# Two graph attention layers with a mixture of experts: five unread products ahead of each pair of lookups

## The chip, the cores and the metric
The kernel runs on one core of one Trainium2 chip. The metric is the device time in microseconds (us), median of several runs. TensorE does matrix products (MATMUL, each with a weight load, LDWEIGHTS), VectorE and ScalarE elementwise work, GpSimd gathers rows by indirect DMA, SyncE issues the other DMAs. Products are written to PSUM, eight banks of 512 float32 columns.

## The reference
```python
x = x + gnn(layernorm(x), edge_index, ...)    # graph 1: 6250 nodes, 100000 edges, 8 heads
x = x + ffn(layernorm(x), ...)                # graph 2, and four experts of which two count

# ffn: scores from a second graph attention over 131072 edges and self loops
e = leaky_relu(a_src[src] + a_dst[dst]); ee = exp(e - e_max[dst])
alpha = ee / segment_sum(ee, dst)[dst]
agg = segment_sum(h[src] * alpha, dst)        # 16 values a node: 4 heads x 4 experts
scores = layernorm(agg).mean(over heads); w = softmax(top 2 of scores)
for ei in range(4):
    out += g[ei] * (gelu(x @ W1[ei] + b1[ei]) @ W2[ei] + b2[ei])   # 256 -> 512 -> 256
```

## The kernel before
The kernel goes through graph 1's features and edges, a middle part that makes graph 2's node table, graph 2's edge stage, and an output stage. Only graph 2's edge stage is touched (`p_edges2` on TensorE, and its partners `v_edges2`, `a_edges2`, `g_edges2`, `sp_edges2` on the other engines).

Graph 2's edges lie in 656 chunks of 128. A round is `W2` = 16 chunks, so there are 41 rounds; `CH` is 4 and u = 0 to 3 names a quarter of a round. Each round has 16 slots, and every engine runs the same loop over rounds and slots, each with its own instructions, ordered by semaphore counts. Into the slots, besides the edge work, the steps of the experts' feed-forward network are dealt out evenly (`ffn_at`): an "up" product (float32, 512 columns, L1354) of which two make the input of one GELU on ScalarE (L858), and a "down" tile (four float32 products of 256 columns, L1368), which VectorE evacuates three slots later (`LATE` = 3, L2570) with the count v_y. A down tile waits until the tile before last is evacuated. The node groups are of 4 tiles, the last one of 1 tile, whose up products have 128 columns.

The edge work of round i on TensorE:
- in each slot one sum product for a chunk of round i - 2 (L1398, bfloat16, 60 columns), which needs VectorE's one-hot matrices (v_oh, L2581) and messages (v_ms);
- in slots 8 and 12, twice a round, `lookups` for two quarters of round i: per chunk one bfloat16 product of 24 columns (L1382) that gives each edge its destination's terms, eight products a time. They are written to columns 0 to 383 of bank i % 2. They need table rows that ScalarE copied in the round before (a_tw, L872), one-hot matrices that VectorE made of rows loaded by DMA (v_st, L2590, at its slots 0 and 4), and the bank, free once VectorE has read it for round i - 2 (v_z, the score at L2596).

GpSimd gathers a chunk's 128 source rows per instruction (L728), up to three rounds ahead, and every four chunks waits for TensorE's sums. VectorE adds the sums into the accumulator (L2642). SyncE stores the evacuated tiles (L512) and loads the destination rows (L519).

`ident` and `ones` are float32 128x128 constants in SBUF. All float32 products appear in the trace as two MATMULs and two LDWEIGHTS each.

Of the kernel before, what the change touches and what calls it, by code (L numbers as in the profile page):

```python
# [42 lines left out]
def build(nc, x_d, src_d, dst_d, W_d, as_d, ad_d, bias_d, lns_d, lnb_d, Wg_d, gas_d, gad_d, bg_d, gam_d, bet_d,  # L43
# [8 lines left out]
    with ctx:  # L52
        def sb(name, shape, dt=f32):
            return ctx.enter_context(nc.sbuf_tensor(name, shape, dt))

        def pb(name, shape, dt=f32):
            return ctx.enter_context(nc.psum_tensor(name, shape, dt))
# [4 lines left out]
        def sems(names):  # L62
            return [sem(n) for n in names.split()]
# [68 lines left out]
        ident = sb("ident", [128, 128])  # L132
        ident16 = sb("ident16", [128, 128], b16)
        tri = sb("tri", [128, 128])
        ones = sb("ones", [128, 128])
# [52 lines left out]
        pbank = [pb(f"pb{i}", [128, 512]) for i in range(8)]  # L188
# [149 lines left out]
        def wait_read(e, n):  # L338
# [19 lines left out]
        l_d1, s_dlT, v_oT, p_tp, a_w32, p_ad, v_z, a_ex, v_msg, p_sum, v_add = sems(  # L358
            "l_d1 s_dlT v_oT p_tp a_w32 p_ad v_z a_ex v_msg p_sum v_add")
# [113 lines left out]
        def ffn_at(n):  # L473

            return [op for s in ffn_steps[taken[n]:taken[n + 1]] for op in s] if n >= 0 else []
# [867 lines left out]
        def p_ffn(pe, op):  # L1343
            if op[0] == "up":
                _, bi, f, k = op
                ei, gi = blk[bi]
                t0, nt = groups[gi]
                n, w, b = 4 * bi + f, ei % 2, 5 + (4 * bi + f) % 2
                if k == 0:
                    if f == 0 and gi == 0:  # L1350
                        pe.wait_ge(l_w1[w], 32 * (ei // 2 + 1))
                    if n >= 2:
                        pe.wait_ge(a_gel, n - 1)
                t = pe.matmul(pbank[b][:, 0:nt * 128], W1s[:, w, k, f * 128:f * 128 + 128],  # L1354
                              xT[:, t0:t0 + nt, k * 128:k * 128 + 128], start=k == 0, stop=k == 1)
                if k == 1:
                    t.then_inc(p_up, 1)
            if op[0] == "down":
                _, bi, j = op
                ei, gi = blk[bi]  # L1360
                n, w = downs[(bi, j)], ei % 2
                b = (4, 7)[n % 2]
                if n >= 2:
                    pe.wait_ge(v_y, n - 1)
                for f in range(4):
                    if j == 0:
                        pe.wait_ge(a_gel, 4 * bi + f + 1)
                    t = pe.matmul(pbank[b][:, 0:D], hh[:, bi % 2, f, j * 128:j * 128 + 128], W2s[:, w, f, :], start=f == 0, stop=f == 3)  # L1368
                t.then_inc(p_dn, 1)

        def p_edges2(pe, m, lo, hi, base, fill):
            nf = 0

            def lookups(n):
                i, u = divmod(n, 4)
                r = i - base
                pe.wait_ge(m["a_tw"], n - 4 * base + 1)
                pe.wait_ge(m["v_st"], 2 * r + u // 2 + 1)
                if r >= 2:
                    pe.wait_ge(m["v_z"], 4 * (r - 2) + 1)  # L1380
                for k in range(u * CH, u * CH + CH):
                    t = pe.matmul(pbank[i % 2][:, 24 * k:24 * k + 24], ST2[:, k // 8, k % 8, :], tabw[:, i % 2, 24 * k:24 * k + 24],  # L1382
                                  start=True, stop=True)
                t.then_inc(m["p_ad"], 1)

            for i in range(lo, hi + 2):
                for u in range(4):
                    for k in range(CH):
                        c = (i - 2) * W2 + u * CH + k
                        if c >= lo * W2:  # L1390
                            rc = c - base * W2
                            if u == 0 and k == 0:
                                pe.wait_ge(m["v_ms"], 6 * (i - 2 - base) + 6)
                            if k == 0:
                                pe.wait_ge(m["v_oh"], 4 * (i - 2 - base) + u + 1)
                            if rc >= 16 and rc % 8 == 0:
                                pe.wait_ge(m["v_wh"], rc // 8 - 1)
                            pe.matmul(pbank[2 + c // 8 % 2][:, c % 8 * 60:c % 8 * 60 + 60], S2[:, i % 2, u * CH + k, :],  # L1398
                                      Mb[i % 2][:, u * CH + k, :, :], start=True, stop=True).then_inc(m["p_sm"], 1)
                        if k == 0 and u >= 2 and i < hi:  # L1400
                            lookups(4 * i + 2 * u - 4)
                            lookups(4 * i + 2 * u - 3)
                        if fill:
                            for op in ffn_at(nf):
                                p_ffn(pe, op)
                            nf += 1

        def tensor_program(pe):
# [107 lines left out]
            for step in ffn_steps[0:PRE2]:  # L1516
                for op in step:
                    p_ffn(pe, op)
            p_edges2(pe, main2, 0, ROUNDS, 0, True)


# [1209 lines left out]
```

## Time and profile before

| | us |
|---|---|
| time, median of 3 runs (2254.3 to 2259.53) | 2255.82 |
| profiled execution, span from first to last instruction | 2627.5 |
| profiled execution, its own time beside the span | none is given; the span stands for it |
| TensorE, MATMUL busy in the span | 1983.2 |
| VectorE busy | 1730.8 |
| GpSimd busy | 1554.8 |
| ScalarE busy | 871.5 |
| graph 2's edge stage, about | 1505 to 2521 |

The profiled execution is 372 us longer than the median of the runs. Times in the rows are of the profiled execution. Engines are named PE (TensorE matmul), PEld (its weight loads), DVE (VectorE), ACT (ScalarE), POOL (GpSimd) and SP (SyncE); an "L" and a number is the line of the kernel. "Idle before" is the time that an engine did nothing ahead of an instruction, with what released it; "issue" is time in which it waited for nothing that the profile shows, "remote" a release that no instruction of the trace accounts for.

### The profile page before, as it was taken

Reading aid. Unit: us, or ns where it says so; the run is one execution under the profiler, and the core shown is the slowest. Engines: PE = TensorE matmul, PEld = TensorE weight load, DVE = VectorE, ACT = ScalarE, POOL = GpSimd, SP = SyncE. Lnnn points to the kernel's source line nnn. Section 1 sums busy time; section 2 is a strip of 40 time slices with the busy share of each in tenths; the row PEclk is TensorE's granted clock in tenths of the full one; section 3 lists DMA queues with packets and bytes.
Section 4 is the critical chain, followed back from the end, with each engine's and each line's share of the span. In section 5 each row is a group of like instructions: output and inputs, shape, how many; then the busy total and the mean of one; then the engine's idle time right before and its main releaser. Section 6 shows DMA issues by size and latency. Waiting matters only on the chain.

```text
span 2627.5 us, 36265 instructions
## 1 busy us (share of the span) xinstructions
PE 1983.2 (75%) x10396; PEld 1276.1 (49%) x10396; DVE 1730.8 (66%) x4885; ACT 871.5 (33%) x2296; POOL 1554.8 (59%) x1720
## 2 busy tenths in 40 slices
PE   7577675677778677777777668788788788888857
PEld 5243354445445444544545435454455455555536
DVE  6588897778888888888599225444444454454568
ACT  6311111333333333333266323333323233233225
POOL 2666676666666666667464546666565666566600
PEclk9789987899999899998778679899888998899978
DMA  7434444434434443434600112222122222221137
GB/s 211 129 101 111 111 121 111 113 107 108 113 108 108 113 111 106 112 108 111 201 5 7 26 48 60 55 75 58 47 55 70 54 63 63 51 38 35 32 125 272
DMA packets 147851, 239.99 MB, mean 91 GB/s; under 512 B 39734, under 2 KB 79332, under 8 KB 147652
## 3 DMA queue, kind: packets, MB, share of 16 engines
q0 software_dynamic: 58624, 116.81, 18.7%
q1 hardware_dynamic: 89028, 120.82, 14.8%
q8 instruction: 89, 1.46, 0.2%
q14 instruction: 110, 0.90, 0.1%
HBM read 203.79 MB, written 33.72 MB: 90 GB/s over the span
## 4 chain that ended last, share of the span: by engine, by line
PE 43%; DVE 17%; issue 15%; another core or an unknown queue 15%; ACT 4%; DVEq 2%; POOL 1%; DMA 1%; ACTq 1%; SPq 0%
PE pb L1451 9%; PE pb L1368 8%; PE pb L1354 8%; PE pb L1341 5%; PE pb L1333 2%; DVE x_sb L2497 1%; PE pb L1438 1%; PE pb L1529 1%; DVE Gb L1665 1%; PE pb L1299 1%; DVEq L2636 1%; DVE home L2642 1%; DVE x_sb L2406 1%; ACT x_sb L848 1%
## 5 line engine op out<-in xcount | busy, mean ns | idle before, releaser
L775 POOL DMA_INDIRECT Gb<-table,home x400 | 411.3, 1028 | 217.3 <-issue 95.2
L1368 PE MATMUL pb<-Gb,early 128*128 128x256 f32 x1568 | 436.1, 424 | 87.4 <-DVE home L2570 39.5
L1354 PE MATMUL pb<-big,Gb 128*128 128x512 f32 (+1 forms) x832 | 444.1, 648 | 70.0 <-issue 38.6
L1368 PEld LDWEIGHTS pb<-Gb,early 128*128 128x128 f32 x1568 | 311.7, 209 | 190.9 <-issue 79.5
L2497 DVE TENSOR_SCALAR x_sb<-iota,x_sb 128x394 bf16<-128x394 f16 x1024 | 349.2, 385 | 42.4 <-PE pb L1341 19.9
L858 ACT ACTIVATE early<-pb,b1c 128x512 f32<-128x512 f32 (+1 forms) x208 | 136.8, 662 | 634.9 <-remote 349.4
L1341 PE MATMUL pb<-x_sb 128*128 128x394 bf16 x1024 | 296.6, 349 | 12.8 <-DVE x_sb L2497 7.2
L728 POOL DMA_INDIRECT home<-table,idx x224 | 216.5, 966 | 151.2 <-issue 62.4
L2570 DVE TENSOR_TENSOR home<-pb,b2B 128x256 f32<-128x256 f32 x147 | 62.0, 422 | 363.1 <-remote 291.6
L728 POOL DMA_INDIRECT tab<-table,idx x224 | 219.1, 978 | 137.9 <-issue 61.2
L848 ACT ACTIVATE x_sb<-pb 128x512 f16<-128x512 f32 x256 | 153.0, 598 | 368.4 <-remote 151.9
L728 POOL DMA_INDIRECT early<-table,idx x208 | 200.0, 962 | 126.7 <-issue 55.6
L1451 PE MATMUL pb<-Gb,Sall 128*128 128x264 f32 x800 | 261.9, 430 | 7.2 <-DVE Gb L1665 3.6
L775 POOL DMA_INDIRECT home<-table,home x192 | 197.4, 1028 | 96.4 <-issue 47.5
L775 POOL DMA_INDIRECT early<-table,home x192 | 201.7, 1050 | 86.8 <-issue 48.9
L965 ACT CAST Sall<-pb 128x1024 f32<-128x1024 bf16 x98 | 99.1, 1012 | 350.3 <-PE pb L1438 188.8
L1354 PEld LDWEIGHTS pb<-big,Gb 128*128 128x128 f32 x832 | 135.9, 204 | 160.2 <-issue 122.8
L1333 PE MATMUL pb<-x_sb 128*128 128x512 f16 x256 | 104.4, 408 | 103.7 <-issue 46.8
L1451 PEld LDWEIGHTS pb<-Gb,Sall 128*128 128x128 f32 x800 | 159.9, 212 | 41.9 <-issue 11.8
L2642 DVE TENSOR_TENSOR home<-home,asall 128x20 f32 x656 | 116.1, 178 | 96.4 <-issue 50.7
L1665 DVE TENSOR_TENSOR Gb<-Gb 128x512 f32<-128x512 f32 x200 | 133.8, 685 | 33.3 <-ACT Gb L969 20.5
L1341 PEld LDWEIGHTS pb<-x_sb 128*128 128x128 f16 x1024 | 101.3, 102 | 101.3 <-DVE x_sb L2497 27.7
(455 smaller groups left out, 3590.5 us busy)
## 6 DMA issues: line engine op xcount, KB each, us to landing
Sall<-dlT SPq DMA_DIRECT2D x180, 256.0 KB
Y<-home SPq DMA_DIRECT2D x72, 256.0 KB
x_sb<-in_x_dram SPq DMA_DIRECT2D x5, 1536.0 KB, 20.2
Gb<-table,home POOLq DMA_INDIRECT x400
early<-Y SPq DMA_DIRECT2D x8, 768.0 KB, 5.7
out_dram<-x_sb SPq DMA_DIRECT2D x24, 256.0 KB
Gb<-Y SPq DMA_DIRECT2D x6, 768.0 KB, 8.6
Gb<-in_L_ffn_W_dram SPq DMA_DIRECT2D x8, 512.0 KB
```

The source lines that it names most:

```text
L728: g.indirect_dma_start(out=Gt2[s][:, k, :], out_offset=None, in_=g2.table, in_offset=bass.IndirectOffsetOnAxis(ap=g2.idx[:, c:c + 1], axis ...
L775: g.indirect_dma_start(out=G1[i % 4][:, k, :], out_offset=None, in_=g1.table, in_offset=bass.IndirectOffsetOnAxis(ap=g1.idx[:, c:c + 1], a ...
L848: a.activation(Av[g % 4], hot_bank[:, :], ACT.Relu).then_inc(a_av, 1)
L858: a.activation(hh[:, bi % 2, f, 0:nt * 128], pbank[b][:, 0:nt * 128], ACT.Gelu, bias=b1c[:, ei, f:f + 1]).then_inc(a_gel, 1)
L1333: pe.matmul(hot_bank[:, :], CT[g // 4 % 2], lanes[:, g % 4 * 512:g % 4 * 512 + 512], start=True, stop=True).then_inc(p_hot, 1)
L1341: pe.matmul(pbank[5 + 2 * w][:, 0:HW], A, Bv[n], start=j % HB == 0, stop=j % HB == HB - 1).then_inc(p_pl, 1)
L1354: t = pe.matmul(pbank[b][:, 0:nt * 128], W1s[:, w, k, f * 128:f * 128 + 128], xT[:, t0:t0 + nt, k * 128:k * 128 + 128], start=k == 0, stop ...
L1368: t = pe.matmul(pbank[b][:, 0:D], hh[:, bi % 2, f, j * 128:j * 128 + 128], W2s[:, w, f, :], start=f == 0, stop=f == 3)
L1451: pe.matmul(sbank[m % 3][:, 0:g1.R], S1[:, i % 2, k, :], G1[(i - 2) % 4][:, k, :], start=c % RUN == 0, stop=c % RUN == RUN - 1).then_inc(p ...
L1665: v.tensor_tensor(hv, hv, G1[e % 4][:, o, 256:264].unsqueeze(3).broadcast_to([128, 2, 8, 32]), ALU.mult).then_inc(v_msg, 1)
L2497: v.tensor_scalar(Bv[j % NB], iota16[:, 0:HW], winF[:, k:k + 1], bE[:, k:k + 1], ALU.is_equal, ALU.mult).then_inc(v_bv, 1)
L2642: v.tensor_tensor(o, o, sums2[c // 8 % 2][:, c % 8, :], ALU.add).then_inc(m["v_ad"], 1)
```

## The change
A helper `p_turn_over` does n float32 products of 128 columns, `ident` by `ones`, into columns 384 to 511 of a bank, which nothing reads. `lookups` calls it with n = 5 for u = 0 and u = 2, that is once ahead of each of the two sets of eight lookups in a round, on the bank that the lookups are about to write. The wait for the bank (v_z) is moved ahead of the products; the waits for the tables (a_tw) and the one-hot matrices (v_st) now come behind them. No semaphore is signalled by the products.

```diff
+        def p_turn_over(pe, bank, n):
+
+            for k in range(n):
+                pe.matmul(bank[:, 384:512], ident[:, :], ones[:, :], start=True, stop=True)
+
         def p_edges2(pe, m, lo, hi, base, fill):
             nf = 0
 
             def lookups(n):
                 i, u = divmod(n, 4)
                 r = i - base
+                if r >= 2:
+                    pe.wait_ge(m["v_z"], 4 * (r - 2) + 1)
+                if u in (0, 2):
+                    p_turn_over(pe, pbank[i % 2], 5)
                 pe.wait_ge(m["a_tw"], n - 4 * base + 1)
                 pe.wait_ge(m["v_st"], 2 * r + u // 2 + 1)
-                if r >= 2:
-                    pe.wait_ge(m["v_z"], 4 * (r - 2) + 1)
```

## Rows read from the trace of the kernel before

**Rows 1.** The page: span, busy times, granted clock in 40 slices (tenths)
```profile
span 2627.5 us, 36265 instructions
PE 1983.2 (75%) x10396; PEld 1276.1 (49%) x10396; DVE 1730.8 (66%) x4885; ACT 871.5 (33%) x2296; POOL 1554.8 (59%) x1720
...
PEclk9789987899999899998778679899888998899978
```

**Rows 2.** Windows: busy us (instructions) per engine, granted clock, DMA
```profile
1505.00:2521.00 1016.00, 833.60 (x3607) 512.82 (x3606) 470.46 (x1518) 328.56 (x960) 606.61 (x627) 0.89 0.23 52
```

**Rows 3.** The chain that ended last, 1505 to 2521 us, by line
```profile
by line: another core or an unknown queue 24.6%; PE pb L1354 20.8%; PE pb L1368 20.6%; issue 14.3%; DVEq L2636 2.2%; DVE home L2642 2.2%; ACT early L858 1.9%; PE pb L1382 1.0%; PE pb L1398 1.0%; ACT dl L872 1.0%; DVE home L2570 0.9%; DVE Sa
```

**Rows 4.** TensorE's waits, 1505 to 2521 us: total, times, longest
```profile
PE pb L1382 <- issue: 40.1, 30, 2.6
PE pb L1368 <- DVE home L2570: 39.5, 17, 6.8
```

**Rows 5.** Timeline of TensorE from 1522 us: start, us, what, idle before
```profile
1522.39 0.18 PE L1382 MATMUL pb<-dl,STb 128*128 128x24 bf16 x1 [2.62 <-issue]
...
1525.19 0.18 PE L1382 MATMUL pb<-dl,STb 128*128 128x24 bf16 x1 [2.62 <-issue]
```

**Rows 6.** Waits of all engines, 1505 to 2521 us: the longest two
```profile
ACT early L858 <- remote: 349.4, 58, 18.1
DVE home L2570 <- remote: 291.6, 42, 29.0
```

**Rows 7.** Timeline of TensorE, 1909 to 1928 us
```profile
1909.95 1.10 PE L1354 MATMUL pb<-big,Gb 128*128 128x512 f32 x2
1910.89 0.19 PE L1398 MATMUL pb<-iota,Sall 128*128 128x60 bf16 x1
...
1911.89 1.97 PE L1368 MATMUL pb<-Gb,early 128*128 128x256 f32 x8
1913.70 0.19 PE L1398 MATMUL pb<-tmr,Sall 128*128 128x60 bf16 x1
...
1923.88 3.78 PE L1368 MATMUL pb<-Gb,early 128*128 128x256 f32 x8 [4.07 <-DVE home L2570]
...
1927.53 0.39 PE L1382 MATMUL pb<-dl,STb 128*128 128x24 bf16 x8
```

**Rows 8.** Timeline of the other engines in the same stretch
```profile
1912.51 0.95 POOL L728 DMA_INDIRECT early<-table,idx  x1 [0.30 <-issue]
...
1923.40 0.42 DVE L2570 TENSOR_TENSOR home<-pb,b2B 128x256 f32<-128x256 f32 x1 [7.91 <-remote]
1923.56 0.69 ACT L858 ACTIVATE early<-pb,b1c 128x512 f32<-128x512 f32 x1 [5.04 <-remote]
1923.72 0.95 POOL L728 DMA_INDIRECT early<-table,idx  x1 [2.76 <-remote]
```

**Rows 9.** Groups by line and form in the stage; one line's durations and starts
```profile
L1368 PE MATMUL pb<-Gb,early 128*128 128x256 f32 x1523 | 425.7, 425 | 87.4 <-DVE home L2570 39.5 <-issue 28.3 <-DVE big L2570 9.9
L1354 PE MATMUL pb<-big,Gb 128*128 128x512 f32 x743 | 418.4, 674 | 40.0 <-issue 25.6 <-ACT early L858 14.3
...
L1354 PE MATMUL pb<-big,Gb 128*128 128x128 f32 x64 | 12.1, 326 | 11.0 <-ACT early L858 7.5 <-issue 3.5
...
L728 POOL DMA_INDIRECT tab<-table,idx x215: 941/947/1472, 1499.6 to 2499.9; - x108
```

**Rows 10.** Timelines with TensorE's float32 products of 128 columns
```profile
1750.36 1.20 PE L1354 MATMUL pb<-big,Gb 128*128 128x128 f32 x4
...
2516.38 0.19 PE L1398 MATMUL pb<-tmr,Sall 128*128 128x60 bf16 x1
2516.41 0.35 PE L1382 MATMUL pb<-dl,STb 128*128 128x24 bf16 x8
2516.61 0.69 PE L1354 MATMUL pb<-big,Gb 128*128 128x128 f32 x4
2517.14 0.19 PE L1398 MATMUL pb<-tmr,Sall 128*128 128x60 bf16 x1
```

## The prediction
> **What bounds the kernel now.** I read the page first: TensorE is busy 75% of the span, more than VectorE (66%) or GpSimd (59%), and the granted clock changes all along the span [rows 1]. An average over unlike stages says little, so next come the busy times by stage. The change acts only in graph 2's edge stage, 1505 to 2521 us. There TensorE is busy 833.6 of 1016 us, GpSimd 606.6, VectorE 470.5, at a mean granted clock of 0.89 [rows 2]. TensorE is the engine with least room, and 182 us of idle time is all the cover there is.
>
> Is that idle time where the products go, ahead of the lookups? The waits say: TensorE's idle time ahead of L1382 is 40.1 us in 30 pieces, and none is ended by a semaphore of ScalarE (a_tw) or VectorE (v_st); all is "issue" [rows 4]. The timeline shows what "issue" is: within one set of four or eight lookups, where nothing is waited for, single instructions come 2.80 us apart (1522.39, 1525.19) [rows 5]. Products ahead of the set can't fill gaps inside it. TensorE's waits on a semaphore are elsewhere, at the down products (L1368) for VectorE, 39.5 us in 17 pieces [rows 4].
>
> The chain of the stage gives 24.6% to "another core or an unknown queue" [rows 3], though one core runs. The waits name it: ScalarE's GELU waits 349.4 us and VectorE's evacuation 291.6 us for something without a releaser [rows 6]. The timeline shows one such case. TensorE begins the down product at 1911.89 and the next instruction at 1913.70, so it is through with it; VectorE, which evacuates it three slots later, starts only at 1923.40, ScalarE's GELU at 1923.56 and GpSimd's gather at 1923.72 [rows 7, 8]. Three engines that wait for three different TensorE counts go on within 0.32 us. So TensorE's completion signals reached them some 8 us late, and TensorE itself then stood 4.07 us for want of the evacuation [rows 7]. I read the stuttered issue and the late signals as one fault of TensorE's sequencer in this execution.
>
> That matters for how the profile stands to the clocked runs. The span is 2627.5 us, the median 2255.82: the profiled execution is 372 us (14%) longer. My terms are durations of warm, unstuttered stretches; the waits are what I trust least. If the 372 us come off evenly, the stage lasts 1016 x 2256/2627.5 = 872 us in a clocked run. A floor comes from GpSimd: 627 gathers [rows 2] at a start-to-start of 1.25 us [rows 8] are 784 us, and 21 us lie between its last gather at 2499.9 [rows 9] and the stage's end: 805 us. What TensorE must do at full clock, from start-to-start times: 743/2 = 371.5 up products of 512 columns x 0.94 us = 349; 1523/8 = 190 down tiles x 1.81 us = 345; 64/4 = 16 short pairs x 0.53 = 8; 656 sums x 0.03 = 20; 82 sets of eight lookups x 0.20 = 16 [rows 7, 9, 10]. Together 738 us. So in a clocked run TensorE has 67 to 134 us in the stage that it doesn't need, part of it idle and part of it lost at the low clock.
>
> **The change, part by part.** *The products.* W2 is 16 and there are 656/16 = 41 rounds, in each of which `lookups` is called with u = 0, 1, 2, 3; u = 0 and 2 issue five products each: 82 times five, 410 calls. A float32 call is two MATMULs and two LDWEIGHTS (the code has 32 short up calls in the stage, the trace 64 MATMULs of them [rows 9]), so 820 and 820 instructions. The same form stands in the trace: the last group's up products are float32 128x128 on 128 columns. Four MATMULs, two calls, go from 2516.61 to the next instruction at 2517.14, 0.53 us; a call is 0.265 us, five are 1.33 us. At the lower clock the four last 1.20 us instead of 0.69 (1750.36), five calls by that ratio 2.3 us [rows 10]. So 82 x 1.33 = **109 us** at full clock. Were 22% of them at 1.2 GHz (a granted mean of 0.89 between 1 and 0.5), 82 x (0.78 x 1.33 + 0.22 x 2.3) = 127 us. Bounds: by columns alone, from the 512-column call, 0.94/4 = 0.235 us a call and 96 us in all; with no overlap at all between instructions, the 0.326 us that a short MATMUL lasts on the mean [rows 9] ten times for each of 82 sets, 267 us. I take 109, since its row has the same form; ident and ones instead of activations change no size.
>
> The trace puts the cost of a short float32 MATMUL with its weight load at 0.13 us [rows 10]. The Trainium skill ("TensorE: Matmul & The Clock Gate", LDWEIGHTS) has a load take columns divided by 1.2 GHz, 107 ns here, pulled ahead of matmuls in flight. By that two loads bound a call at 0.21 us, and the sum would be 88 us instead of 109; the measured row decides.
>
> *The moved wait.* v_z is now waited for ahead of a_tw and v_st, and ahead of the products. It asks for the score of the round before last. VectorE makes the score of the last round in its slot 2, ahead of the evacuation of slot 3 that stands at 1923.40 [rows 8], and TensorE's next lookups come at 1927.53 [rows 7]; the score asked for is a whole round earlier still. Nothing waits: 0 us. Unread columns 384 to 511 of the same bank are written while VectorE reads, if at all, the other bank: 0 us.
>
> *The order.* The products stand ahead of the waits for a_tw and v_st, so they would cost nothing where TensorE waits there for over 1.3 us. No such wait is in the trace [rows 4], and the slots say why: TensorE asks for v_st at slots 8 and 12, VectorE issues the one-hots at its slots 0 and 4, and the tables were copied a round before. A VectorE more than eight slots late holds up TensorE earlier, at a down product, as it does at 1923.88 [rows 7]. So the products are pure work in TensorE's order. Behind them stand the lookups, the next sum and the next feed-forward step; the lookups' count is wanted by VectorE's score in the next round, and 1.3 us don't show there.
>
> *What absorbs them.* Delayed TensorE work eats idle time of its own that hangs on others (gathers, evacuations), not what is serial. Per round 2.7 us of products meet 67/41 = 1.6 to 134/41 = 3.3 us of room. With the stage at 805 us and half its 67 us of room of use, +109 - 34 = +75; all of it, +42; none, +109. With the stage at 872 us and half, +42; all, 847 against 872, nothing. Half of the smaller room is my choice, as the profiled execution's long waits are mostly its own: **+75 us, 2256 + 75 = 2331 us**, with 2290 to 2370 for this case.
>
> **The rivals.**
> *The clock repays it (faster).* The low clock comes after stalls, and in the stage it takes 22% of the time; what is lost by it is 0.11 x 1016 = 112 us here, 96 us scaled to a clocked run. If the products kept the clock up throughout and half of them lay in idle time, the sum would be -96 + 55 = -41, **2215 us**. It decides once more than 109 us less the hidden part comes back. For it: TensorE's low clock is real in the rows, 3.78 us for a down tile after a stall where a warm one takes 1.97 [rows 7]. Against it: the stalls of the trace lie ahead of down products, and the products come slots later. [...]
> *Absorbed (about the same).* GpSimd or late evacuations set the pace, with 872 us or more to the stage, and TensorE's 109 us go into its idle time: -5 to +25, **2265 us**. For it: 182 us of idle in the stage [rows 2]; against it: 14% of the span isn't there in clocked runs.
> *Dearer products.* Weight loads that don't overlap, 267 us less 34: +233, **2489 us**. Against it, the 0.53 us row.
>
> **How the numbers follow.** Likeliest case 0.70, clock 0.12, absorbed 0.13, dearer 0.05. Range 2255 to 2380: it takes in the likeliest case with 10 us above it and nearly all of the absorbed one, and leaves out the clock and the dearer case, under 2 in 10. No difference means within 0.2%, 4.5 us, about what can be told here: the absorbed case puts 0.05 within it and 0.08 above, and the others 0.01: faster 0.12, same 0.06, slower 0.82.
>
> **What would show it.** In the changed kernel's profile: 820 more short MATMULs, five calls in 1.3 us when warm, right behind the previous feed-forward step without idle time ahead of them; no semaphore wait ahead of L1382's successor; TensorE's busy time in the stage up by 100 to 130 us; the stage itself longer by half of that or more. The prediction is wrong if the granted clock of the stage rises from 0.89 to near 1 and the stage shrinks, or if busy time rises by 110 us and the time doesn't, which would make the real room far larger than 67 us.

## The result and the profile after

The changed kernel takes 2287.31 us against 2257.33 for the kernel before, medians of four runs each: a ratio of 1.0139, 95% interval 1.0117 to 1.0161, or +30 us. The direction is the forecast one and the time lies in the range, but the forecast step was +75 us, 2.5 times what came.

Of the page of the changed kernel, two of the lines that answer to [rows 1]:

```profile
span 2278.9 us, 37905 instructions
PE 1942.1 (85%) x11216; PEld 1290.0 (57%) x11216; DVE 1726.2 (76%) x4885; ACT 877.7 (39%) x2296; POOL 1568.6 (69%) x1720
```

The span is now 2 us below this execution's own time of 2280.76. There are 820 more MATMULs, 11216 instead of 10396. The profiled execution that the prediction rests on was 372 us longer than its kernel's clocked runs, so the two spans can't be compared. The kernel before was therefore profiled once more among the experiments. Its second profile has a span of 2244.8 us at a time of 2246.71, and all "before" below means that one.

The edge stage by windows, from some 2 us ahead of the first lookups to some 3 us behind the last, first the kernel before, then the changed one (columns as in [rows 2]):

```profile
1336.00:2140.00 804.00, 756.85 (x3624) 479.42 (x3623) 468.25 (x1523) 333.77 (x965) 611.98 (x631) 0.98 0.26 66
```
```profile
1336.00:2173.00 837.00, 836.62 (x4439) 567.67 (x4440) 478.96 (x1522) 332.33 (x960) 621.47 (x635) 1.00 0.27 64
```

The stage takes 33 us longer, and that is the whole difference. Before, TensorE is idle for 804 - 757 = 47 us of it, and the granted mean of 0.98 says that a little of the rest went at the lower of its two clocks. In the changed kernel it has no idle time and the full clock from end to end.

The chain of the stage, by line, the kernel before and the changed one:

```profile
by line: PE pb L1368 24.1%; PE pb L1354 23.2%; issue 20.3%; POOL early L728 9.6%; POOL home L728 9.1%; POOL tab L728 6.8%; PE pb L1382 1.2%; PE pb L1398 1.1%; DVEq L2636 0.9%; DVE home L2642 0.6%; DVE home L2570 0.5%; DVE big L2596 0.2%; AC
```
```profile
by line: PE pb L1354 42.7%; PE pb L1368 40.8%; PE pb L1374 11.6%; PE pb L1405 2.1%; PE pb L1389 1.8%; issue 0.2%; ACT L884 0.2%; ACTq L868 0.1%; DVE asall L2636 0.1%; DVE home L2649 0.1%; DVE early L2630 0.1%; DVE early L2626 0.1%; DVE home
```

Before, a quarter of the chain is GpSimd's gathers and a fifth is "issue": the 0.30 us from one gather to the next, and a wait of VectorE for the last gather of a round, which the next view shows. Afterwards it is TensorE alone, with 11.6% for the products (L1374; by the added lines L1382 is now L1389, L1398 is L1405, L2570 is L2577 and L2601 is L2608).

What a round of the kernel before waits for, in its timeline over all engines:

```profile
1715.74 0.19 PE L1398 MATMUL pb<-tmr,Sall 128*128 128x60 bf16 x1
...
1717.01 0.94 POOL L728 DMA_INDIRECT tab<-table,idx  x1 [0.30 <-issue]
...
1720.40 0.23 DVE L2601 TENSOR_TENSOR zc<-tab,big 128x64 f32<-128x64 f32 x1 [7.37 <-issue]
...
1722.40 0.42 DVE L2570 TENSOR_TENSOR home<-pb,b2B 128x256 f32<-128x256 f32 x1
...
1722.88 3.35 PE L1368 MATMUL pb<-Gb,early 128*128 128x256 f32 x7 [6.95 <-DVE home L2570]
```

GpSimd issues a round's last gather into `tab` at 1717.01. VectorE's score (L2601), the first reader of these rows, starts at 1720.40, 2.45 us after that gather has ended and after 7.37 us of waiting. "issue" in its row is no name of a releaser; that it is the gathers follows from the count (l_g) for which the code waits there, and from the experiments below, in which the wait grows with a slower GpSimd and is gone with fewer gathers. The evacuation behind it in VectorE's order comes at 1722.40, and TensorE, which ran out of allowed work at 1715.9, goes on at 1722.88. TensorE stands in slot 2 there. The products come in slots 8 and 12, so not in the wait itself; they only make TensorE come later to a place at which it had to wait for GpSimd. No run puts them in another slot.

The same wait in the groups of waits over the stage, the kernel before and then the changed one:

```profile
DVE zc L2601 <- issue: 89.6, 15, 7.4
DVE zb L2601 <- issue: 83.9, 16, 6.5
POOL home L728 <- issue: 61.3, 201, 0.3
```
```profile
DVE home L2577 <- PE pb L1368: 169.0, 100, 5.6
```

VectorE waited 173 us for gathers, in 31 of the rounds; now it waits for TensorE's down tiles, and no longer for gathers. In the first seven rounds of the kernel before it didn't wait for gathers either, because GpSimd starts ahead: the score comes 14 us behind its last gather at first, and 3 us in the seventh round. From the eighth on (1495 us) the head start is used up. GpSimd itself has no pause of more than 0.3 us ahead of a gather in this window, and its last gathers, in the kernel before and then in the changed one, start at nearly the same time (each line has the durations in ns, then the first and the last start in us):

```profile
L728 POOL DMA_INDIRECT tab<-table,idx x224: 940/944/1302, 1330.7 to 2146.2; - x112
```
```profile
L728 POOL DMA_INDIRECT tab<-table,idx x224: 941/947/1456, 1329.0 to 2149.8; - x112
```

So five products don't slow GpSimd; it is no longer what the stage waits for.

What one set of products costs, in TensorE's timeline of the changed kernel:

```profile
2163.87 1.36 PE L1374 MATMUL pb<-ones,ident 128*128 128x128 f32 x10
...
2165.07 0.35 PE L1389 MATMUL pb<-dl,STb 128*128 128x24 bf16 x8
```

Five products go from 2163.87 to 2165.07, 1.20 us, with no idle time in front; the mean of all 82 sets is 1.19. 82 x 1.20 = 98 us.

### The profile page after: what moved, and what is told of

It is laid out like the page before. It is cut to its first block, busy times and chain, and to the rows that moved or that the text cites. A ratio compares the mean times of both kernels' runs of the same rounds, so it can differ in the third digit from the quotient of the medians.

```text
span 2278.9 us, 37905 instructions
## 1 busy us (share of the span) xinstructions
PE 1942.1 (85%) x11216; PEld 1290.0 (57%) x11216; DVE 1726.2 (76%) x4885; ACT 877.7 (39%) x2296; POOL 1568.6 (69%) x1720
## 4 chain that ended last, share of the span: by engine, by line
PE 51%; DVE 20%; POOL 13%; issue 9%; DMA 5%; DVEq 1%; ACT 1%; ACTq 0%; SPq 0%
PE pb L1354 16%; PE pb L1368 15%; POOL Gb L775 6%; PE pb L1374 4%; PE pb L1458 3%; DVE x_sb L2504 3%; POOL home L775 3%; POOL early L775 3%; DMA Gb<-table,home 2%; PE pb L1341 2%; DVE Gb L1672 2%; PE pb L1536 2%; PE pb L1155 2%; DVE big L1636 1%; DVE x_sb L2413 1%
## 5 line engine op out<-in xcount | busy, mean ns | idle before, releaser
L775 POOL DMA_INDIRECT Gb<-table,home x400 | 419.4, 1048 | 126.5 <-issue 106.4
L1354 PE MATMUL pb<-big,Gb 128*128 128x512 f32 (+1 forms) x832 | 410.5, 608 | 10.5 <-DVE home L1796 9.6
L1368 PE MATMUL pb<-Gb,early 128*128 128x256 f32 x1568 | 385.3, 389 | 0.4 <-DVE home L2577 0.2
L2504 DVE TENSOR_SCALAR x_sb<-iota,x_sb 128x394 bf16<-128x394 f16 x1024 | 343.6, 384 | 0.0
L1368 PEld LDWEIGHTS pb<-Gb,early 128*128 128x128 f32 x1568 | 283.2, 190 | 81.9 <-issue 49.4
L1458 PE MATMUL pb<-Gb,Sall 128*128 128x264 f32 x800 | 248.6, 412 | 16.9 <-DVE Gb L1672 16.7
L2577 DVE TENSOR_TENSOR home<-pb,b2B 128x256 f32<-128x256 f32 x147 | 62.2, 423 | 180.8 <-PE pb L1368 180.8
L1458 PEld LDWEIGHTS pb<-Gb,Sall 128*128 128x128 f32 x800 | 152.0, 203 | 44.8 <-DVE Gb L1672 18.9
L1354 PEld LDWEIGHTS pb<-big,Gb 128*128 128x128 f32 x832 | 126.5, 192 | 84.3 <-issue 67.2
L1458 PE MATMUL pb<-early,Sall 128*128 128x264 f32 x384 | 120.1, 416 | 13.9 <-DVE early L1672 13.9
```

The source lines that it names most:

```text
L775: g.indirect_dma_start(out=G1[i % 4][:, k, :], out_offset=None, in_=g1.table, in_offset=bass.IndirectOffsetOnAxis(ap=g1.idx[:, c:c + 1], a ...
L1458: pe.matmul(sbank[m % 3][:, 0:g1.R], S1[:, i % 2, k, :], G1[(i - 2) % 4][:, k, :], start=c % RUN == 0, stop=c % RUN == RUN - 1).then_inc(p ...
L2504: v.tensor_scalar(Bv[j % NB], iota16[:, 0:HW], winF[:, k:k + 1], bE[:, k:k + 1], ALU.is_equal, ALU.mult).then_inc(v_bv, 1)
```

## The experiments

Three theories were put to the test. Theory A: GpSimd's gathers set the pace of the stage before, TensorE has some 66 us of room at full clock (804 less the 738 us of work counted in the prediction), the products fill it first, and cost their full time beyond. Theory B: a fixed share of each product is serial, which gives the same 30 us at five. Theory C, that the clock repays part of the products, would show with few of them.

**The kernel before, profiled again** (no edit).

> The kernel before, profiled once more. Theory A (GpSimd's gathers set the pace of graph 2's edge stage, and TensorE has some 70 us of idle time there at full clock): a profile without the stuttered issue and the late signals, span near 2256 us, the stage about 805 us long, GpSimd's gathers at an even 1.22 us, TensorE busy some 730 us at a granted clock of 1.0, its idle time in small pieces once a round ahead of a down product or a sum. Theory B (TensorE's own serial chain sets the pace, with cold stretches): the same span, but a granted clock in the stage well below 1 and GpSimd with idle time of its own.

One run, 2246.71 us. The profile is the one used above: no stuttered issue, gathers mostly 1.25 us apart (0.94 and 0.30 of it between) and 1.27 on the mean, where 1.22 was expected, TensorE idle for 47 us, nearly all of it in 27 waits at down tiles. That is theory A's picture with two misses: TensorE is busy 757 us and not 730, at a clock of 0.98 and not 1.0, which is still not well below 1; and its idle time is in fewer and longer pieces, up to 6.9 us.

**Other numbers of products.** The wait is moved in all of them; n is 0, 2, 3, 4, 5 or 10. They ran in three groups, each with its own runs of the kernel before.

```diff
-                    p_turn_over(pe, pbank[i % 2], 5)
+                    p_turn_over(pe, pbank[i % 2], 10)
```

> The wait for the bank moved ahead and no products. Every theory: no difference that can be measured, within 0.2%; if the moved wait had a price of its own, it would show here.

> Two products ahead of each set of lookups instead of five: 82 x 2 x 0.266 = 44 us more work for TensorE than in the kernel before. Theory A: all of it goes into the idle time of some 70 us, 2257 us, within 0.3% of the kernel before. Theory B (a fixed share of each product is serial, as 30 us of 109 were measured for five): 2/5 of 30, +12 us, 2269 us. Theory C (the clock repays part): 5 to 20 us faster than before.

> Three products ahead of each set. TensorE's work at full clock is 738 us and the stage of the kernel before 804, so 66 us are free, 0.8 us a set. Theory A with products at 0.23 us (five measured at 1.20 with their start): three cost 0.72 a set, 59 us, all absorbed: within 0.3% of the kernel before. Theory B: 3/5 of 30, +18 us.

> Four products ahead of each set: 0.96 us a set, 79 us against 66 free. Theory A: +13 us, between 8 and 18, the knee. Theory B: 4/5 of 30, +24 us.

> The changed kernel itself, on the same chip as three and four products. Theory A: 98 - 66 = +32 us over before. The step from four to five is then a full product, 19 us, where the step from three to four is 6 to 13 and that from none to three nothing; by theory B all steps are 6 us.

> Ten products ahead of each set: 218 us more work for TensorE than before. Theory A: TensorE is already the bound with five, so five more cost their full 109 us: 2287 + 109 = 2396 us. Theory B: a fixed share, +60 us, 2317 us.

| products a set | us | before, us | ratio, 95% interval | theory A | theory B |
|---|---|---|---|---|---|
| 0 | 2246.35 | 2247.16 | 0.9997, 0.9984 to 1.0011 | 0 | 0 |
| 2 | 2246.51 | 2244.92 | 1.0004, 0.9990 to 1.0019 | 0 | +12 |
| 3 | 2250.01 | 2249.86 | 1.0007, 0.9996 to 1.0018 | 0 | +18 |
| 4 | 2260.71 | 2249.86 | 1.0057, 1.0041 to 1.0073 | +13 | +24 |
| 5 | 2281.62 | 2249.86 | 1.0147, 1.0127 to 1.0166 | +32 | +30 |
| 10 | 2366.46 | 2244.92 | 1.0540, 1.0510 to 1.0570 | +139 | +60 |

By the ratios nothing up to three, +13 us at four, +33 at five, +121 at ten: a knee where the room ends. From three to four products the medians rise by 11 us, where 6 to 13 were expected, and from four to five by 21, where 19 were. Theory B falls at two, three, four and ten. Theory C falls at two products, which are not faster, and the moved wait has no price. Only the 139 us at ten were too much. The timeline of that kernel shows why:

```profile
1706.47 2.48 PE L1374 MATMUL pb<-ones,ident 128*128 128x128 f32 x20
1708.78 0.35 PE L1389 MATMUL pb<-dl,STb 128*128 128x24 bf16 x8
```

Ten take 2.31 us, 0.23 each, and not the 0.266 that I had still used: 82 x 2.31 = 189, less 66, is 123 us, against 121 measured.

The windows of the stage with three, four and ten products show TensorE filling up:

```profile
1338.00:2147.00 809.00, 802.67 (x4111) 532.30 (x4112) 472.44 (x1523) 333.13 (x962) 617.36 (x629) 1.00 0.28 66
```
```profile
1336.00:2156.00 820.00, 818.60 (x4275) 549.59 (x4276) 478.37 (x1522) 332.68 (x961) 616.86 (x635) 1.00 0.28 65
```
```profile
1334.00:2261.00 927.00, 927.00 (x5258) 659.01 (x5257) 480.13 (x1522) 331.48 (x956) 616.74 (x633) 1.00 0.23 57
```

**Fewer gathers.** Every fourth gather of the edge stage is left out from round 3 on, in the kernel before and in the changed one; a quarter of the source rows are stale there.

```diff
                 for k in range(W2):
...
+                    if i >= 3 and k % 4 == 3:
+                        continue
                     g.indirect_dma_start(out=Gt2[s][:, k, :], ...)
-                v.wait_ge(m["l_g"][i % 3], 16 * W2 * (len([...])))
+                v.wait_ge(m["l_g"][i % 3], 16 * (W2 + 12 * (i // 3)))
```

> The kernel before with every fourth gather of the edge stage left out from round 3 on (152 of 656), so that a quarter of the source rows are stale. Theory A: GpSimd's pace falls from 784 to about 600 us, TensorE's 730 to 740 us become the bound, the stage falls from some 805 to 750 to 770 us: 2205 to 2220 us. Theory B: GpSimd isn't the pace, within 10 us of 2257.

> The changed kernel with every fourth gather left out from round 3 on, a quarter of the source rows stale. Theory A: TensorE was the bound in both, so leaving gathers out gains nothing here, and the products cost their full 82 x 1.20 = 98 us over the same kernel without products (a ratio of 0.973 to the kernel before): a ratio of 1.010 to 1.018. Theory B: about 30 us over it, a ratio near 0.986.

Without products 2182.88 us, a ratio of 0.9727 (0.9699 to 0.9755), -62 us: more than the 37 to 52 expected, but close to the 66 us of room. With products 2278.50, 1.0140 (1.0112 to 1.0168), no faster than the changed kernel with all its gathers. So in the changed kernel GpSimd isn't the bound at all, and with GpSimd out of the way five products cost 0.0413 x 2247 = 93 us instead of 30. (The two ratios are of two groups of runs.) Theory B's ratio of 0.986 is excluded. The stage without products and with fewer gathers:

```profile
1330.00:2072.00 742.00, 738.46 (x3617) 469.75 (x3616) 475.21 (x1521) 333.28 (x965) 474.37 (x484) 1.00 0.27 69
```

TensorE's own work is 738 us, the very sum of the prediction, in a stage of 742. VectorE's waits for gathers are gone. With the products added it is this window of the changed kernel with fewer gathers, TensorE 98 us busier in a stage 95 us longer:

```profile
1332.00:2169.00 837.00, 836.37 (x4437) 567.48 (x4438) 475.86 (x1522) 332.62 (x961) 466.86 (x483) 1.00 0.25 61
```

**A slower GpSimd.** Two memsets of a scratch tile a round on GpSimd, in the kernel before and in the changed one. They last 734 ns on the mean in the trace.

```diff
                     g.indirect_dma_start(...).then_inc(m["l_g"][s], 16)
+                    if k % 8 == 2:
+                        g.memset(spin[:, :], 0.0).then_inc(*gc.one())
+                        g.wait_ge(*gc.now())
```

> The kernel before with two memsets of a scratch tile of 640 columns a round on GpSimd in the edge stage, estimated at 0.6 to 0.7 us each with their semaphore (from the memset of 1707 columns at 1.6 us), 41 x 1.4 = 57 us on GpSimd's queue. Theory A (GpSimd sets the pace before): all of it shows, +45 to +60 us over the kernel before, and TensorE's idle time grows by as much. Theory B (it doesn't): under +15 us.

> The same two memsets a round in the changed kernel. Theory A: GpSimd's pace is now longer than TensorE's work with the products, so these cost nothing: within 8 us of the kernel before with the same memsets. Theory B (a fixed share of each product is serial): 30 us over it.

Both are 1.0261 of the kernel before (1.0230 to 1.0291 without products, 1.0232 to 1.0289 with them), +59 us. With GpSimd slower by some 1.4 us a round, the same five products cost nothing. This is the sharpest case against B, whose 30 us would have been 0.013. In the waits over the stage of the first, TensorE stands for VectorE's evacuation longest, and VectorE for the gathers; with products both are shorter:

```profile
PE pb L1372 <- DVE home L2574: 48.1, 23, 8.4
...
DVE zc L2605 <- issue: 131.2, 18, 9.1
```
```profile
PE pb L1372 <- DVE home L2581: 12.6, 5, 6.9
...
DVE zc L2612 <- issue: 69.9, 13, 9.0
```

## Why the prediction was wrong in size

*The step that failed* is the last one of the sum, that "half of the smaller room" is absorbed. The smaller room itself came out right: 67 us, where 66 are measured (804 - 738). But all of it absorbs products, not half. The stage was said to last 805 us if GpSimd sets the pace; it lasts 804. The prediction had that case in the text, "all of it, +42", and passed over it. The reason for a half was the mistrust of the long waits of that execution, and this is no reason: once 805 us is GpSimd's pace, TensorE's room below it is by construction idle time that hangs on another engine, and all of it takes work. What was missing was the check of one against the other: max(805, 738 + 109) = 847 us against 805. It would have given +42 us and 2298.

That 805 and 804 us agree so closely is partly luck. The sum took 1.25 us a gather and 21 us behind the last one. In the second profile the window holds 631 gathers at 1.27 us on the mean, as some last up to 1.4 us, which is 15 us more; and the last gather starts 6 us behind the window's end, so the 21 us aren't there.

*The term of the products* was too dear by 11 us: 109 was forecast and 98 measured, since ten MATMULs in a row take 0.120 us each, where the row of the same form [rows 10] gave 0.133 with a sum product behind. The prediction's lower bound by columns alone, 96 us, was the nearer one. With 98 us and the whole room, 98 - 66 = +32, against 30 measured. So of the 45 us too much, 32 are the absorption and 11 the price; the rest is what a sum of this kind can't hold.

*What was right.* The demand of TensorE, 738 us, is the 738.46 us of the run in which nothing else bound it. The moved wait costs nothing (0.9997). Nothing is waited for at the lookups, and the products are not hidden there. The reading that the stuttered issue and the waits without a releaser belonged to that execution is borne out: in the stage of the second profile no wait is marked "remote" and TensorE has no "issue" wait, and its span agrees with its time. That TensorE's signals came late, and that this was one fault of its sequencer, is not shown; no run here looked for the cause.

*The wait at the down tile.* The prediction read VectorE's 291.6 us without a releaser [rows 6] as late signals. In the clean profile VectorE waits for the gathers ahead of the score instead, and this is the evidence that GpSimd sets the pace. The first profile couldn't give it: VectorE's score (L2601) has not one wait there. GpSimd was ahead in it and stood itself, once for 21.0 us, for VectorE to free the rows' buffer.

*The rivals.* The clock: the granted clock rises from 0.98 to 1.00 in the stage, not from 0.89, and what it gives back, 804 less 738 of work and 47 of idle time, some 19 us, is part of the 66 us of room. So of the 98 us of products 47 went into idle time, 19 came back through the clock, and 32 are left. TensorE's busy time in the stage rises by 80 us (757 to 837) for the same reason, and not by the 100 to 130 that were to show. After the wait of 6.95 us above, seven MATMULs of a down tile take 3.35 us where eight take 1.97 warm [rows 7], so the low clock is real; but the time lost in it lay in GpSimd's shadow as well: two or three products give no gain, and with fewer gathers the clock is at 1.00 without any product. The absorbed case is the right mechanism up to three products and wrong at five, as the room ends at 66 us. Products without overlap, 0.326 us a MATMUL, didn't come. The Trainium skill ("TensorE: Matmul & The Clock Gate", LDWEIGHTS) puts a load of 128 columns at 107 ns; the 0.120 us measured for each load with its product lies nearer to it than my row did.

## What to carry to other kernels

Work added to an engine that waits for another's pace is free until the two are level and costs its full time from there: compare the larger of the two sums before and after, and don't take a share. For that, sum each engine's own work at its undisturbed pace, and count the gaps between instructions on a gathering engine as work; GpSimd's busy share of 76% here was a queue without a hole. And where a profiled execution is much longer than the clocked runs, take durations from it but no waits, and profile the kernel again before reading from waits which engine sets the pace: here the wait that told it was absent from the first profile.

## What had not been expected of the hardware

One execution of the same kernel was 372 us longer than its clocked runs, with single TensorE instructions 2.80 us apart and with VectorE, ScalarE and GpSimd going on within 0.32 us of each other after waits of 7.91, 5.04 and 2.76 us that no instruction of the trace ended; a second profile had none of it. Where VectorE waits for a round's gathers, it goes on 1.4 us after the last of them has ended in most rounds (1697.62 to 1699.04), and 2.45 us in the round shown above. Ten float32 MATMULs of 128 columns in a row take 0.120 us each with their weight loads, and twenty take 0.116.
